# A Mamba-2 and attention block: segment sums taken as differences of running sums in one fp32r pass, and one convolution input projected later

## The chip, the cores and the metric

The kernel runs on one NeuronCore of a Trainium2 chip. The metric is the device time of one execution in microseconds (us), the median of several runs; lower is better. Five engines work side by side, each with its own instruction queue, and meet only through semaphores: TensorE (PE, with its weight loads as PEld), VectorE (DVE), ScalarE (ACT), GpSimd (POOL) and SyncE (SP, which here only issues DMAs).

## The reference

For each of 8 sequences of 512 tokens with 128 channels, after one layer norm, two branches are computed and joined as `x + s * silu(f)`:

```
s branch: h = layernorm(x); z, xBC, dt = h @ in_proj          (256 | 384 | 4 columns)
          xBC = silu(conv4(xBC)); xs, B, C = xBC;  dt = softplus(dt + bias)
          per head:  H_t = exp(dt_t * A) H_(t-1) + dt_t x_t B_t;   y_t = H_t C_t + D x_t
          y = rmsnorm(y * silu(z)) @ out_proj; + residual; then layernorm and a GELU MLP
f branch: rmsnorm, causal attention with 16 heads of 8 channels, then 4 experts, the top 2 weighted
```

The recurrence over t is done in 4 chunks of 128 tokens. Inside a chunk, with the running sum `S_t = sum of dt_k * A for k up to t` of one head, the weight of source token s for target token t is `exp(S_t - S_s)` for s up to t, times `C_t . B_s`. The exponent `S_t - S_s` is what the code calls the segment sum. There are 4 heads, so one chunk has a 128 x 512 tile of segment sums (source token on the partitions, head and target token on the free axis).

## The kernel before, in words

One sequence is one round. `stage_b(r, tail, head)` ends round r (its "tail": output projections, MLP, experts) and begins round r+1 (its "head": qkv, convolution and gate projections, maxima of the attention scores), interleaved by hand. `stage_a` then does the attention and the scan of the new round. The program is `stage_b(-1)` with head only, `stage_a`, seven loop rounds of `stage_b` and `stage_a`, and a last `stage_b` with tail only. The order of work on every engine is the order written in the code.

`stage_a` walks 24 units `e`, six (`u` = 0 to 5) for each of 4 quarters `g`. A unit is a slice of the attention scores: PE computes it (`exp_scores`, or two at once in `exp_scores_of_four`), ACT exponentiates it (`exponentiate`, L1097) into `pr`, POOL masks it (L1715), PE multiplies it with the values three units later (`weigh_values`). In quarter 0 the last maxima of the scores are still found: PE writes `max_scores`, DVE reduces them (`maxima`, L1194). The scan of chunk g is woven between: `segments` and `scan_inputs` at u = 1 (at e = 2 for chunk 0), then ACT's exponential of the segment sums into `es` (L1132), DVE's `scan_weights` (`wm`, L1474), PE's `scan_outputs` at u = 4.

Segment sums before: POOL's `decays(c)` (L1699) builds `rs`, 128 x 512, with row k, head h, column t holding `dta[k, h]` if k is at most t and else 0; `decays(0)` stands ahead of unit 0, the others at u = 3 of quarters 0 to 2. PE then multiplies with the constant `after` (1 where k > s), in fp32:

```
mm(R[1][:, :], after, rs[:, c % 2].rearrange("p h t -> p (h t)")).then_inc(seg_ps, 1)
```

In this trace every fp32 product of TensorE stands as two matmul instructions, and an fp32r or bf16 product as one. The running sums for the other uses come from `cumulate`, three small products into `S[0]` near the end of `stage_b`; ACT's exponential of them is `dec` (L1120). After `cumulate` PE does `experts_down(0)`, then `exp_scores(0)`, `max_scores` and so on; `experts_down(t)` uses the PSUM bank `R[(22 + t) % 4]`, so t = 3 uses `R[1]`, the bank of the segment sums. `rs` shares its memory with `h2a`, an expert's hidden activations.

At the start of `stage_b` PE's order is: qkv products, turning of `ao`, `project_x(0)`, the `wo` product, `project_x(1)`, `project_x(2)`, `project_z(0)`, `project_z(1)`, turning of `x1n`, `project_z(2)`, turning of `xf`, `project_z(3)`, gate logits, and 32 transposes of `tokqk` (L449). `project_x(n)` makes convolution input n, which ACT's `evac_xc(n)` copies out; ACT does `evac_xc(2)` after the squares and the root for `xf`.

Of the kernel before, what the change touches and what calls it, by code (L numbers as in the profile page):

```python
# [93 lines left out]
def build(nc, x, weights, vectors, rows, consts, out):  # L94
    with ExitStack() as ctx:
# [83 lines left out]
        rs = sb("rs", [P, 2, NH, P])  # L179
        es = sb("es", [P, 2, NH, P])  # L180
        gm = sb("gm", [P, 2, P])
# [30 lines left out]
        h2a = rs[:].rearrange("p k h t -> p k (h t)")  # L212
        h2b = es[:].rearrange("p k h t -> p k (h t)")
        h1a = wm[:].rearrange("p k h t -> p k (h t)")
        h1 = sb("h1", [P, 2, L])
        h3a = sb("h3a", [P, L])
# [55 lines left out]
        cum_ps = signal("cum_ps", 1)  # L272
        seg_ps = signal("seg_ps", T)
# [31 lines left out]
        dec_sb = signal("dec_sb", 1)  # L305
        seg_sb = signal("seg_sb", T)
# [29 lines left out]
        sv_sb = signal("sv_sb", 1)  # L336
        moe_sb = signal("moe_sb", T * E)
# [19 lines left out]
        rs_sb = signal("rs_sb", T)  # L357
# [84 lines left out]
        def _(pe):  # L442
# [128 lines left out]

            def segments(r, c):

                pe.wait_ge(rs_sb, at(rs_sb, r, c + 1))
                if c == 0:
                    pe.wait_ge(moe_sb, at(moe_sb, r, 4 * E))
                elif c == 1:
                    pe.wait_ge(h_sb, at(h_sb, r, 1))
                else:
                    pe.wait_ge(h_sb, at(h_sb, r, 2 * c - 1))  # L580
                mm(R[1][:, :], after, rs[:, c % 2].rearrange("p h t -> p (h t)")).then_inc(seg_ps, 1)
# [114 lines left out]
            def stage_b(r, tail, head):  # L696
# [36 lines left out]
                if head:  # L733
                    project_x(r, 1)
                    project_x(r, 2)
# [8 lines left out]
                if head:  # L744
                    project_z(r, 2)
# [95 lines left out]
                if head:  # L841
                    exp_scores(r, 0)
# [54 lines left out]
            pe.wait_ge(pool_set, 10)  # L897
            pe.wait_ge(dve_set, 7)
# [13 lines left out]
        def _(act):  # L912
# [201 lines left out]
            def stage_a(r, tail):  # L1114
# [37 lines left out]
            act.wait_ge(pool_set, 3)  # L1152
            act.preload_act_table_set(EXP_LN)
# [17 lines left out]
        def _(dve):  # L1171
# [145 lines left out]
            def stage_b(r, tail, head):  # L1317
# [91 lines left out]
                if tail:  # L1409
                    for n in range(2):  # L1410
# [7 lines left out]
                       ALU.add).then_inc(sv_sb, 1)  # L1418
                for t in range(T):
# [11 lines left out]
                    if head and t < 2:  # L1431
                        maxima(r, MAX_AT[t])

# [117 lines left out]
            dve.wait_ge(dve_set, 3)  # L1551
# [7 lines left out]
            dve.wait_ge(dve_set, 7)  # L1559
# [17 lines left out]
        def _(pool):  # L1577
# [80 lines left out]
            def time_steps(r):  # L1658
# [29 lines left out]
                pool.sem_inc(pool_passed, 1)  # L1688
                pool.wait_ge(rs_sb, at(rs_sb, r, 0))
# [3 lines left out]
            def decays(r, c, tail):  # L1693

                pool.wait_ge(dt_sb, at(dt_sb, r, DT_STEPS))
                if c == 0 and tail:
                    pool.wait_ge(up_ps, at(up_ps, r, 9))
                pool.wait_ge(seg_ps, at(seg_ps, r, c - 1))
                tt(rs[:, c % 2], upto.unsqueeze(1).broadcast_to([P, NH, P]),  # L1699
                   dta[:, c, :].unsqueeze(2).broadcast_to([P, NH, P]), ALU.mult).then_inc(rs_sb, 1)  # L1700

            def stage_a(r, tail):
                decays(r, 0, tail)
                for e in range(G * UNITS):
# [21 lines left out]
                    if u == 3 and g < T - 1:  # L1726
                        decays(r, g + 1, tail)
# [12 lines left out]
            pool.memset(xc[:, :, 0:3], 0.0).then_inc(pool_set, 1)  # L1740
            pool.memset(cT[:], 0.0).then_inc(pool_set, 1)
# [8 lines left out]
            pool.wait_ge(dve_set, 7)  # L1750
# [71 lines left out]
```

## Time and profile before

| | us |
|---|---|
| median of 3 runs | 872.43 |
| lowest, highest | 872.13, 874.5 |
| the profiled execution, its own time | 876.48 |
| its span (first to last instruction) | 874.8 |
| PE busy | 796.5 |
| DVE busy | 605.7 |
| ACT busy | 496.4 |
| POOL busy | 365.4 |

The profiled execution took 4 us more than the median; 1.7 us of it lie around the span. Busy times of PE are modelled, and a matmul's duration holds its way through the array, so the durations of two neighbours overlap. Start times are counted from the start of the span. The mean granted clock of TensorE over the span is 0.981 of 2.4 GHz.

### The profile page before, as it was taken

The page shows a single profiled execution, that of the slowest core. Times are in us where ns is not written, and L with a number is a line of the kernel's source. Part 1 is how long each engine was busy: PE and PEld are TensorE (multiplying, and loading weights), DVE is VectorE, ACT ScalarE, POOL GpSimd, SP SyncE. Part 2 cuts the span into 40 slices and gives each one's busy share as a digit, 9 for nine tenths or more (in the row PEclk, how much of TensorE's full clock was granted, in tenths as well). Part 3 has the DMA queues.
Part 4 walks back from the last instruction along what each step waited for, and adds up shares of the span by engine and source line. Part 5 has one row for each costly group of instructions (what it writes and reads, how often), then busy time and mean ns, then how long its engine had stood idle before and what let it go on. Part 6 is the DMA issues. An engine that isn't in the chain of part 4 may idle for free. (4 is left out here: it accounts for less than half of the span.)

```text
span 874.8 us, 18230 instructions
## 1 busy us (share of the span) xinstructions
PE 796.5 (91%) x5472; PEld 492.2 (56%) x5472; DVE 605.7 (69%) x1443; ACT 496.4 (57%) x952; POOL 365.4 (42%) x656
## 2 busy tenths in 40 slices
PE   2789999999999999999899999999999998999897
PEld 1554564755647556565647555475555656475555
DVE  2576469784787757786687847877587866878534
ACT  2325774467743675547744678436854577446652
POOL 5633627054541627227280454516272272804500
PEclk9897999999999998999999999999999999999999
DMA  4000000000000100000000000000000000000000
GB/s 163 1 3 18 14 1 1 9 16 25 0 1 6 33 5 0 7 12 25 0 0 7 13 24 0 1 7 26 11 0 7 12 26 0 0 7 13 24 1 13
DMA packets 15145, 11.73 MB, mean 13 GB/s; under 512 B 1040, under 2 KB 13968, under 8 KB 14992
## 3 DMA queue, kind: packets, MB, share of 16 engines
q1 hardware_dynamic: 15120, 11.43, 4.3%
q8 instruction: 12, 0.20, 0.1%
q14 instruction: 13, 0.11, 0.0%
HBM read 7.76 MB, written 2.10 MB: 11 GB/s over the span
## 5 line engine op out<-in xcount | busy, mean ns | idle before, releaser
L1097 ACT ACTIVATE sb_pr<-S 128x768 f32<-128x768 f32 (+1 forms) x192 | 165.8, 890 | 130.8 <-PE S L444 130.8
L1194 DVE TENSOR_REDUCE sb_mx<-S 128x2 f32<-128x256 f32 (+3 forms) x256 | 197.7, 816 | 41.7 <-PE S L444 41.1
L1715 POOL TENSOR_SCALAR_AFFINE_SELECT sb_pr<-sb_pr 128x256 f32<-128x256 f32 (+1 forms) x192 | 98.9, 517 | 292.7 <-ACT sb_pr L1097 289.4
L444 PE MATMUL R<-sb_pr,sb_va 128*32 128x512 f32 (+3 forms) x1024 | 89.7, 445 | 0.0
L444 PE MATMUL S<-sb_kT,sb_qT 32*128 32x256 f32 (+3 forms) x512 | 56.8, 386 | 19.7 <-DVE sb_mx L1194 15.8
L444 PE MATMUL R<-sb_W,sb_pr 128*128 128x96 f32 (+1 forms) x512 | 69.5, 276 | 0.0
L444 PE MATMUL R<-sb_xfT,sb_W 128*128 128x512 f32 x144 | 69.2, 602 | 0.0
L444 PEld LDWEIGHTS S<-sb_kT,sb_qT 32*128 32x128 f32 x512 | 27.8, 184 | 73.0 <-DVE sb_mx L1194 65.2
L444 PEld LDWEIGHTS R<-sb_W,sb_pr 128*128 128x128 f32 x512 | 63.5, 192 | 3.8 <-issue 3.5
L1655 POOL TENSOR_TENSOR sb_cv<-sb_cv,sb_cm 128x512 f32<-128x512 f32 x48 | 62.5, 1302 | 4.0
L444 PE MATMUL S<-sb_qT,sb_kT 32*128 32x256 f32 (+3 forms) x512 | 56.8, 387 | 5.6 <-ACT sb_pr L1097 4.8
L1428 DVE SCALAR_TENSOR_TENSOR sb_x<-R,sb_wts,sb_x 128x96 f32<-128x96 f32 x128 | 40.6, 317 | 22.9 <-PE R L444 19.5
L444 PEld LDWEIGHTS S<-sb_qT,sb_kT 32*128 32x128 f32 x512 | 27.6, 184 | 46.1 <-ACT sb_pr L1097 22.1
L444 PE MATMUL S<-sb_maskb,sb_identb 128*128 128x128 bf16 (+1 forms) x384 | 49.6, 242 | 0.0
L962 ACT ACTIVATE sb_pr<-R 128x512 f32<-128x512 f32 x32 | 19.1, 598 | 39.8 <-PE R L444 39.7
L1617 POOL TENSOR_TENSOR sb_qk<-sb_qk,sb_wqk 128x512 f32<-128x512 f32 x8 | 10.2, 1270 | 72.5 <-ACT sb_sq L997 72.5
L449 PE MATMUL S<-sb_cst,sb_tokqk 128*128 128x128 f32 x256 | 38.2, 321 | 2.4 <-DVE sb_tokqk L1380 2.2
L444 PE MATMUL R<-sb_rs,sb_cst 128*128 128x512 f32 x64 | 36.7, 656 | 2.9 <-DVE sb_x L1428 2.9
L1652 POOL TENSOR_SCALAR sb_cm<-sb_xc,sb_vec 128x512 f32<-128x512 f32 x48 | 36.3, 757 | 6.6 <-POOL sb_cv L1655 6.6
L444 PEld LDWEIGHTS R<-sb_pr,sb_va 128*32 128x32 f32 x1024 | 23.6, 108 | 27.2 <-issue 11.1
L449 PEld LDWEIGHTS S<-sb_cst,sb_tokqk 128*128 128x128 f32 x256 | 36.6, 171 | 3.3 <-DVE sb_tokqk L1380 2.6
L1182 DVE RECIPROCAL sb_rden<-R 128x16 f32<-128x16 f32 x32 | 8.2, 257 | 40.0 <-PE R L712 30.6
(216 smaller groups left out, 1711.2 us busy)
## 6 DMA issues: line engine op xcount, KB each, us to landing
sb_xin<-x SPq DMA_DIRECT2D x9, 256.0 KB, 2.7
sb_W<-weights SPq DMA_DIRECT2D x1, 2290.0 KB, 9.9
sb_qT<-sb_mT SPq DMA_DIRECT2D x128, 4.0 KB
sb_xres<-x SPq DMA_DIRECT2D x8, 256.0 KB, 2.8
out<-sb_xres SPq DMA_DIRECT2D x7, 256.0 KB, 2.3
sb_cT<-sb_xact SPq DMA_DIRECT2D x8, 128.0 KB, 2.3
sb_W<-weights SPq DMA_DIRECT2D x1, 514.0 KB, 4.6
sb_cst<-consts SPq DMA_DIRECT2D x1, 328.0 KB, 3.0
```

Source lines behind the costliest of these rows:

```text
L444: return pe.matmul(o, lhsT, rhs, start=start, stop=stop, skip_group_check=True)
L449: i = pe.transpose(o[:, t * P:(t + 1) * P], src(t), ident)
L962: act.activation(dst, R[k % 4][:, :], func, bias=bias).then_inc(act_up, 1)
L1097: act.activation(pr[:, e % 4, :, 0:n], S[pair_of_exp(e)][:, :, 0:n], ACT.Exp).then_inc(p_sb, 1)
L1182: dve.reciprocal(rden[:], view[:, :, :, HD]).then_inc(done, 1)
L1194: o = dve.tensor_reduce(mx[:, n // P - 1, g, heads[0]:heads[1] + 1], found[:, :, at_col:at_col + n], AX.X, ALU.max, negate=True)
L1428: stt(out=x2[:, t, MASKED:D], in0=R[(22 + t) % 4][:, e * OC:(e + 1) * OC], scalar=wts[:, t, e:e + 1], in1=x2[:, t, MASKED:D], op0=ALU.mult ...
L1617: tt(qk[:, :, 0].rearrange("p t h d -> p t (h d)"), qk[:, :, 0].rearrange("p t h d -> p t (h d)"), wqk[:].rearrange("p h d -> p (h d)").un ...
L1652: ts(cm[:], xc[:, n, k:k + L], vec[:, tap:tap + 1], 0.0, ALU.mult, ALU.add).then_inc(conv_pool, 1)
L1655: tt(cv[:, n], cv[:, n], cm[:], ALU.add).then_inc(conv_pool, 1)
L1715: pool.affine_select(out=keep, in_=keep, compare_op=ALU.is_ge, fill=0.0, base=0, pattern=pattern, channel_multiplier=-1)\
```

## The change

The segment sum is now formed as a difference. DVE's `sums_in_parts` takes the running sums that `cumulate` left in PSUM (16 columns: chunk and head), and stores each twice over as a part rounded to fp32r and a rest, into `cs` (128 tokens x 128, 32 columns for a chunk). PE turns `cs` with one transpose (`turn_sums`), so that parts lie on partitions: of each chunk's 32 partitions the first 8 and the next 8 hold the parts. By a scale and a bias per partition ACT makes from it `seg_v` (the parts on the first 8 of each chunk's partitions, ones on the next 8) and four `seg_l[c]` (ones on chunk c's first 8 partitions, the negated parts on its next 8, zero elsewhere); POOL spreads `seg_v` over the heads once, into `seg_r`. A chunk's segment sums are then one fp32r product of `seg_l[c]` and `seg_r`, and a bf16 product that adds the mask (-1e30 where s > t). So PE's `segments` has no operand that is made anew for each chunk, and POOL's four `decays` in a round become one product. `h2a` has memory of its own, `experts_down(3)` waits until ACT has read the turned sums out of `R[1]`, and `project_x(2)` stands after the turning of `x1n`. Six small reductions on DVE and a memset on POOL are added to the setup.

```diff
--- before.py
+++ after.py
-        rs = sb("rs", [P, 2, NH, P])
         es = sb("es", [P, 2, NH, P])
+        cs = sb("cs", [P, T, 32])
+        seg_v = sb("seg_v", [P, P])
+        seg_l = sb("seg_l", [P, T, P], F32R)
+        seg_r = sb("seg_r", [P, NH, P], F32R)
+        seg_low = sb("seg_low", [P, T])
+        seg_high = sb("seg_high", [P, T])
+        seg_sums = sb("seg_sums", [P, 2])
+        seg_head = sb("seg_head", [P, NH])
...
-        h2a = rs[:].rearrange("p k h t -> p k (h t)")
         h2b = es[:].rearrange("p k h t -> p k (h t)")
         h1a = wm[:].rearrange("p k h t -> p k (h t)")
         h1 = sb("h1", [P, 2, L])
+        h2a = sb("h2a", [P, 2, L])
...
+            def turn_sums(r):
+                pe.wait_ge(cs_sb, at(cs_sb, r, 2))
+                pe.wait_ge(act_up, at(act_up, r, 17))
+                pe.transpose(R[1][:, 0:P], cs[:].rearrange("p c k -> p (c k)"), ident).then_inc(csT_ps, 1)
+
             def segments(r, c):
 
-                pe.wait_ge(rs_sb, at(rs_sb, r, c + 1))
+                pe.wait_ge(segl_sb, at(segl_sb, r, 1 + T))
+                pe.wait_ge(segr_sb, at(segr_sb, r, 1))
                 if c == 0:
                     pe.wait_ge(moe_sb, at(moe_sb, r, 4 * E))
                 elif c == 1:
                     pe.wait_ge(h_sb, at(h_sb, r, 1))
                 else:
                     pe.wait_ge(h_sb, at(h_sb, r, 2 * c - 1))
-                mm(R[1][:, :], after, rs[:, c % 2].rearrange("p h t -> p (h t)")).then_inc(seg_ps, 1)
+                mm(R[1][:, :], seg_l[:, c, :], seg_r[:].rearrange("p h t -> p (h t)"), True, False)
+                mm(R[1][:, :].rearrange("p (h t) -> p h t", h=NH), maskb[:],
+                   identb[:].unsqueeze(1).broadcast_to([P, NH, P]), False, True).then_inc(seg_ps, 1)
...
+                if t == 3 and head:
+                    pe.wait_ge(segl_sb, at(segl_sb, r, 1 + T))
...
                 if head:
                     project_x(r, 1)
-                    project_x(r, 2)
                     project_z(r, 0)
                     project_z(r, 1)
                 if tail:
...
                         dense(bank(0)[:, 0:256], 2)
                 if head:
+                    project_x(r, 2)
                     project_z(r, 2)
...
+                    turn_sums(r)
                     exp_scores(r, 0)
                     max_scores(r, MAX_AT[0])
                     mask_scores(r, MAX_AT[0])
...
+                    if e == 0:
+                        act.wait_ge(csT_ps, at(csT_ps, r, 1))
+                        act.wait_ge(segr_sb, at(segr_sb, r, 0))
+                        act.activation(seg_v[:], R[1][:, 0:P], ACT.Identity, bias=seg_sums[:, 1:2],
+                                       scale=seg_sums[:, 0:1]).then_inc(segl_sb, 1)
+                        act.wait_ge(seg_ps, at(seg_ps, r, 0))
+                        for c in range(T):
+                            act.activation(seg_l[:, c, :], R[1][:, 0:P], ACT.Identity, bias=seg_low[:, c:c + 1],
+                                           scale=seg_high[:, c:c + 1]).then_inc(segl_sb, 1)
...
+                if head:
+                    sums_in_parts(r)
...
+            def sums_in_parts(r):
+
+                total = S[0][:, 0, 0:T * NH].rearrange("p (c h) -> p c h", h=NH).unsqueeze(2)\
+                    .broadcast_to([P, T, 2, NH])
+                parts = cs[:, :, 0:16].rearrange("p c (x y h) -> p c x y h", x=2, y=2)
+                dve.wait_ge(dec_sb, at(dec_sb, r, 1))
+                dve.wait_ge(csT_ps, at(csT_ps, r, 0))
+                dve.tensor_copy(parts[:, :, :, 0].bitcast(F32R), total).then_inc(cs_sb, 1)
+                dve.wait_ge(cs_sb, at(cs_sb, r, 1))
+                tt(parts[:, :, :, 1], total, parts[:, :, :, 0], ALU.subtract).then_inc(cs_sb, 1)
...
+            by_part = ident.rearrange("p (c k) -> p c k", c=T)
+            dve.tensor_reduce(seg_low[:], by_part[:, :, 0:8], AX.X, ALU.add).then_inc(dve_set, 1)
+            dve.tensor_reduce(seg_high[:], by_part[:, :, 8:16], AX.X, ALU.add, negate=True).then_inc(dve_set, 1)
+            dve.wait_ge(dve_set, 4)
+            dve.tensor_reduce(seg_sums[:, 0:1], seg_low[:], AX.X, ALU.add).then_inc(dve_set, 1)
+            dve.tensor_reduce(seg_sums[:, 1:2], seg_high[:], AX.X, ALU.add, negate=True).then_inc(dve_set, 1)
+            dve.tensor_reduce(sp[:, 0], by_part[:, :, 0:16].rearrange("p c (m h) -> p c h m", h=NH),
+                              AX.X, ALU.add).then_inc(dve_set, 1)
+            dve.wait_ge(dve_set, 7)
+            dve.tensor_reduce(seg_head[:], sp[:, 0].rearrange("p c h -> p h c"), AX.X,
+                              ALU.add).then_inc(dve_set, 1)
...
-            def decays(r, c, tail):
-
-                pool.wait_ge(dt_sb, at(dt_sb, r, DT_STEPS))
-                if c == 0 and tail:
-                    pool.wait_ge(up_ps, at(up_ps, r, 9))
-                pool.wait_ge(seg_ps, at(seg_ps, r, c - 1))
-                tt(rs[:, c % 2], upto.unsqueeze(1).broadcast_to([P, NH, P]),
-                   dta[:, c, :].unsqueeze(2).broadcast_to([P, NH, P]), ALU.mult).then_inc(rs_sb, 1)
-
             def stage_a(r, tail):
-                decays(r, 0, tail)
+                pool.wait_ge(segl_sb, at(segl_sb, r, 1))
+                pool.sem_inc(pool_passed, 1)
+                pool.wait_ge(seg_ps, at(seg_ps, r, 0))
+                tt(seg_r[:], seg_v[:].unsqueeze(1).broadcast_to([P, NH, P]),
+                   seg_head[:].unsqueeze(2).broadcast_to([P, NH, P]), ALU.mult).then_inc(segr_sb, 1)
...
-                    if u == 3 and g < T - 1:
-                        decays(r, g + 1, tail)
...
+            pool.memset(cs[:], 0.0).then_inc(pool_set, 1)
```

## Rows read from the trace of the kernel before

**Rows 1.** The page: busy time and share, and TensorE's granted clock in 40 slices.
```profile
PE 796.5 (91%) x5472; PEld 492.2 (56%) x5472; DVE 605.7 (69%) x1443; ACT 496.4 (57%) x952; POOL 365.4 (42%) x656
...
PEclk9897999999999998999999999999999999999999
```
**Rows 2.** Groups by line and form, whole span: names, shapes, count, busy us, mean ns.
```profile
L1699 POOL TENSOR_TENSOR sb_rs<-sb_cst,sb_dta 128x512 f32<-128x512 f32 x32 | 33.3, 1039 | 1.2 <-POOL sb_dta L1690 1.1
...
L444 PE MATMUL S<-sb_maskb,sb_identb 128*128 128x128 bf16 x256 | 28.5, 224 | 0.0
...
L444 PE MATMUL S<-sb_maskb,sb_identb 128*128 128x256 bf16 x128 | 21.1, 278 | 0.0
...
L444 PE MATMUL S<-sb_kT,sb_qT 32*128 32x512 f32 x128 | 20.4, 497 | 2.5 <-DVE sb_mx L1194 1.5 <-DVE sb_kT L1388 0.9
...
L444 PE MATMUL S<-sb_kT,sb_qT 32*128 32x384 f32 x128 | 18.3, 445 | 10.9 <-DVE sb_mx L1194 10.0
```
**Rows 3.** Timeline of the middle of a stage_b: start us, us, engine, line, operation.
```profile
547.34 1.88 PE L444 MATMUL R<-sb_rs,sb_W 128*128 128x512 f32 x4
...
549.06 1.02 PE L444 MATMUL R<-sb_x1T,sb_W 128*128 128x512 f32 x2
```
**Rows 4.** Timeline of ACT in quarter 2 of a stage_a; brackets are idle time.
```profile
501.08 1.02 ACT L1097 ACTIVATE sb_pr<-S 128x1024 f32<-128x1024 f32 x1 [2.56 <-PE S L444]
...
503.40 0.62 ACT L937 ACTIVATE sb_oT<-R 128x512 f32<-128x512 f32 x1
503.88 0.63 ACT L1132 ACTIVATE sb_es<-R 128x512 f32<-128x512 f32 x1
...
504.75 1.55 ACT L1097 ACTIVATE sb_pr<-S 128x768 f32<-128x768 f32 x2
506.86 1.51 ACT L1097 ACTIVATE sb_pr<-S 128x768 f32<-128x768 f32 x2 [0.56 <-PE S L444]
```
**Rows 5.** Timeline of PE in the same quarter: the segment sums.
```profile
502.11 1.13 PE L444 MATMUL R<-sb_rs,sb_cst 128*128 128x512 f32 x2
```
**Rows 6.** Timeline from the end of a stage_b through quarter 0, three engines.
```profile
472.53 0.21 ACT L1120 ACTIVATE sb_dec<-S 128x48 f32<-128x48 f32 x1 [3.27 <-PE S L444]
474.74 1.02 ACT L1097 ACTIVATE sb_pr<-S 128x1024 f32<-128x1024 f32 x1 [2.00 <-PE S L444]
...
475.62 1.21 DVE L1194 TENSOR_REDUCE sb_mx<-S 128x2 f32<-128x1024 f32 x1
...
484.60 0.69 DVE L1474 TENSOR_TENSOR sb_wm<-sb_es,sb_gm 128x512 f32<-128x512 f32 x1 [0.30 <-ACT sb_es L1132]
...
486.08 1.12 DVE L1527 TENSOR_SCALAR sb_xn<-sb_xin,sb_mv,sb_lnv 128x128 f32<-128x128 f32 x2
...
482.76 1.10 PE L444 MATMUL R<-sb_rs,sb_cst 128*128 128x512 f32 x2 [0.42 <-DVE sb_x L1428]
```
**Rows 7.** Timeline of PE in the first third of a stage_b.
```profile
533.30 0.66 PE L449 MATMUL R<-sb_cst,sb_xf 128*128 128x128 f32 x4 [1.18 <-DVE sb_xf L1364]
```
**Rows 8.** Timeline of the 32 transposes in two rounds, and ACT's dec in three.
```profile
330.61 6.44 PE L449 MATMUL S<-sb_cst,sb_tokqk 128*128 128x128 f32 x32
...
535.83 3.71 PE L449 MATMUL S<-sb_cst,sb_tokqk 128*128 128x128 f32 x32
...
163.94 0.21 ACT L1120 ACTIVATE sb_dec<-S 128x48 f32<-128x48 f32 x1 [3.27 <-PE S L444]
...
371.20 0.21 ACT L1120 ACTIVATE sb_dec<-S 128x48 f32<-128x48 f32 x1 [3.21 <-PE S L444]
...
778.16 0.21 ACT L1120 ACTIVATE sb_dec<-S 128x48 f32<-128x48 f32 x1 [3.26 <-PE S L444]
```
**Rows 9.** Windows, first round: PE, PEld, DVE, ACT, POOL busy, then granted clock.
```profile
66.00:68.00 2.00, 1.48 (x8) 0.64 (x6) 1.23 (x1) 1.11 (x2) 0.42 (x1) 0.65 0.09 19
...
70.00:72.00 2.00, 2.00 (x8) 1.08 (x8) 1.56 (x5) 0.81 (x1) 0.42 (x2) 0.50 0.00 0
```
**Rows 10.** Timeline of the setup: POOL's last memset.
```profile
7.52 0.39 POOL L1742 MEMSET sb_hst<- 128x256 f32 x1
```

More of the change, by code:

```diff
@@ L272, in build @@
         cum_ps = signal("cum_ps", 1)
+        csT_ps = signal("csT_ps", 1)
         seg_ps = signal("seg_ps", T)
@@ L305, in build @@
         dec_sb = signal("dec_sb", 1)
+        segl_sb = signal("segl_sb", 1 + T)
         seg_sb = signal("seg_sb", T)
@@ L336, in build @@
         sv_sb = signal("sv_sb", 1)
+        cs_sb = signal("cs_sb", 2)
         moe_sb = signal("moe_sb", T * E)
@@ L356, in build @@
         spa_sb = signal("spa_sb", 3)
-        rs_sb = signal("rs_sb", T)
+        segr_sb = signal("segr_sb", 1)
         pm_sb = signal("pm_sb", G * UNITS)
@@ L896, in _ @@
             pe.wait_ge(c_loaded, 48)
-            pe.wait_ge(pool_set, 10)
-            pe.wait_ge(dve_set, 7)
+            pe.wait_ge(pool_set, 11)
+            pe.wait_ge(dve_set, 13)
             pe.wait_ge(xab_sb, at(xab_sb, -2, 1))
@@ L1152, in _ @@
             act.wait_ge(pool_set, 3)
+            act.wait_ge(dve_set, 6)
             act.preload_act_table_set(EXP_LN)
@@ L1548, in _ @@
             dve.tensor_copy(maskb[:], future).then_inc(dve_set, 1)
+            by_part = ident.rearrange("p (c k) -> p c k", c=T)
[9 more added lines that the diff above has]
+                              ALU.add).then_inc(dve_set, 1)
             ts(wqk[:], row[:, R_QN:R_QN + HD].unsqueeze(1).broadcast_to([P, AH, HD]), HD ** -0.5, None,
                ALU.mult).then_inc(dve_set, 1)
-            dve.wait_ge(dve_set, 3)
+            dve.wait_ge(dve_set, 9)
             tt(wqk[:], wqk[:], row[:, R_KN:R_KN + HD].unsqueeze(1).broadcast_to([P, AH, HD]),
@@ L1558, in _ @@
             norms(-2)
-            dve.wait_ge(dve_set, 7)
+            dve.wait_ge(dve_set, 13)
             stage_b(-1, False, True)
@@ L1687, in time_steps @@
                 pool.wait_ge(cum_ps, at(cum_ps, r, 0))
-                pool.sem_inc(pool_passed, 1)
-                pool.wait_ge(rs_sb, at(rs_sb, r, 0))
                 tt(dta[:], dt[:], neg_a[:].unsqueeze(1).broadcast_to([P, T, NH]),
                    ALU.mult).then_inc(dt_sb, 1)
-            def decays(r, c, tail):
-                pool.wait_ge(dt_sb, at(dt_sb, r, DT_STEPS))
-                if c == 0 and tail:
-                    pool.wait_ge(up_ps, at(up_ps, r, 9))
-                pool.wait_ge(seg_ps, at(seg_ps, r, c - 1))
-                tt(rs[:, c % 2], upto.unsqueeze(1).broadcast_to([P, NH, P]),
-                   dta[:, c, :].unsqueeze(2).broadcast_to([P, NH, P]), ALU.mult).then_inc(rs_sb, 1)
-            def stage_a(r, tail):
-                decays(r, 0, tail)
+            def stage_a(r, tail):
+                pool.wait_ge(segl_sb, at(segl_sb, r, 1))
[3 more added lines that the diff above has]
+                   seg_head[:].unsqueeze(2).broadcast_to([P, NH, P]), ALU.mult).then_inc(segr_sb, 1)
                 for e in range(G * UNITS):
@@ L1749, in _ @@
             pool.sem_inc(pool_passed, 1)
-            pool.wait_ge(dve_set, 7)
+            pool.wait_ge(dve_set, 13)
             pool.sem_inc(pool_passed, 1)
```

## The prediction

> **What bounds the kernel.** The page says that PE is busy 91% of the span, far ahead of DVE at 69% and ACT at 57% [rows 1]. Read as a share of the whole, every PE cycle saved would be time saved. So I went to the groups by form, for the cost of the segment product, and then to the timelines of single quarters, to see what is waiting when that product ends.
>
> A round is some 101.3 us: `dec` starts at 371.20 and again at 472.53 [rows 6, 8]. In quarter 2 of a stage_a ACT works from 501.08 to 506.30 (504.75 + 1.55) with no idle bracket: two exponentials, between and behind them the turned y, `oT`, `es` and the squares, then two more exponentials in 1.55 us. The only waits for PE are before the first (2.56 us) and before the next pair at 506.86 (0.56) [rows 4]. The segment product of this quarter runs from 502.11 to 503.24 [rows 5], and its reader `es` starts at 503.88 because `oT` is before it on ACT [rows 4]. It has 0.6 us to spare. So in quarters 1 to 3 this stretch is set by ACT, and PE is busy without being the bound. In quarter 0 the segment product at 482.76 had waited 0.42 us for the last expert sum of DVE, and DVE's `wm` at 484.60 waits 0.30 us for `es` [rows 6]: here the product is nearly on the path. The early part of stage_b is a chain over DVE and ACT, in which PE idles; before the transposes of `xf` it has been idle 1.18 us [rows 7].
>
> **The clock.** The slices show the granted clock below full speed early on and once in the middle [rows 1]. The 32 transposes behind that idle stretch take 3.71 us in the round of 535.83 but 6.44 us in the round of 330.61 [rows 8]: the second ran at 1.2 GHz. Seven `dec`s, the first at 163.94 and the last at 778.16, are 614.2 us apart [rows 8]; six rounds of 101.33 would be 608.0. The other 6.2 us are what the falls of the clock at this place cost in this execution (the transposes above alone account for 2.7 of them). In the first round too the clock falls, in the window from 66 to 68 us, after the stall around the start of stage_a, and is at half from 70 to 72 [rows 9].
>
> **The change part by part.**
>
> *Segment product.* Before: two instructions of 512 columns in fp32. Four such in a row take 1.88 us and two 1.02 [rows 3], so two more cost 0.86 us, which is one product. After: an fp32r instruction of 512 columns grows by 497 - 445 = 52 ns for 128 columns, and a bf16 one by 278 - 224 = 54 ns [rows 2], so 0.21 us each and 0.43 together. The fp32r rows have 32 partitions and not 128; I take the same rate. Bounds for the pair: 0.43, and 0.86 if the full array takes fp32r at half that rate and the two don't overlap well. So 0.43 us of PE time is saved in each of 32 products, 13.7 us in all, and nothing at the far bound. How much is on the path:
> - Quarters 1 to 3 (24 products): 0. ACT's unbroken run hides it; if that cover were gone it would be 24 x 0.43 = 10.3 us.
> - Quarter 0 of the seven loop rounds: `es` comes 0.4 us earlier, `wm` takes up its 0.30 wait, and the maxima behind `wm` on DVE start earlier, until they meet scores that PE has not finished. I read the slack as about 0.13 of 0.30: 7 x 0.13 = 0.9 us. Bounds 0 and 7 x 0.30 = 2.1.
> - Quarter 0 of the first round: at half clock [rows 9] the saving doubles to 0.85 us, and PE goes straight on to the next scores: -0.85.
>
> *`turn_sums`.* One transpose, 3.71 / 32 = 0.12 us [rows 8], ahead of `exp_scores(0)`. It needs the two small DVE operations behind `dec`, which ends at 472.74; taking 0.21 us for each, as `dec` itself has, and a little for two hops, they end at about 473.3. PE is then still in `experts_down(0)`: the scores behind it let ACT start only at 474.74, after 2.00 us idle [rows 6]. The 0.12 us of PE is hidden as well: the second block of maxima waits for DVE's maximum of the first, 475.62 + 1.21 = 476.83 [rows 6], and that does not move. DVE's copies fall into idle time before its first expert sum. So 0 in loop rounds; 7 x 0.12 = 0.8 if the cover fails. In the first round there is no `experts_down(0)` to cover it: `exp_scores(0)`, which ran before `dec`, now waits for `dec`, two DVE operations and a transpose. I put it at +1.0 once (bounds 0.5 and 2, from one small operation's delay to the whole chain at half clock).
>
> *Five small ACT operations* of 128 columns after the first exponential. The nearest rows are `dec` with 48 columns, 0.21 us [rows 6], and `oT` with 512, 0.62 [rows 4]. I take 0.35 each with their two pointers, 1.75 in all (bounds 1.05 and 3.1). The first exponential ends at 475.76 [rows 6], so the second, which now comes behind them, starts at 477.5 (at the far bound 478.9). PE needs it just before the segment product of 482.76 [rows 6]: cost 0. `experts_down(3)`, which now waits for the same copies, ends with the expert sum that DVE adds just before 482.76, and so starts some 3 us earlier, 2 us after the copies.
>
> *POOL.* Four products of 1.04 us [rows 2] become one, behind `seg_v` at about 476.2. POOL's first mask is late by under 2 us; the first product with the values, which needs it, comes after the segment product of 482.76. Less work on POOL could also help DVE: its two `xn` ran beside `rs(1)` and took 1.12 us [rows 6]. No row shows them without a neighbour, so I take 0.06 us a round, 0.4 in all (0 to 1).
>
> *`project_x(2)`*, two instructions, 0.86 us on PE. It leaves a place where PE is early anyway, since next it has to wait for `x1n`, and goes into the 1.18 us before the transposes of `xf` [rows 7]. `evac_xc(2)` on ACT then starts some 0.3 us later; behind it ACT waits for the same transposes of `xf`. By its own time: 0. If ACT had no slack there: 7 x 0.3 = +2.1. But it divides the idle stretch. The falls of the clock come after that stretch, and PE has 0.86 us more work in it now. I take it that about half of the falls go: of the 6.2 us in the profiled execution some 3 to 4, and in the median one, which is 4 us faster than the profiled and so had fewer falls, 2.5. Bounds: 0 and 6.2. No row gives this; it is the weakest term.
>
> The Trainium skill, "TensorE: Matmul & The Clock Gate", Part 1: The HAM clock gate, says that the throttled state is the default and that activity releases it. By that rule the moved product helps here; the trace agrees that the clock falls behind idle PE and nowhere in the dense parts. The same rule speaks against the other half of the change, which takes work away from PE in stage_a (rival C).
>
> *Setup.* A memset of 128 columns on POOL, which is on the chain to the first `xa`: the one of 256 columns takes 0.39 [rows 10], so +0.2 once. The six DVE reductions lie in idle time of DVE.
>
> **The sum.** -0.9 - 0.85 + 1.0 + 0.2 - 0.4 = about -1.0 us without the clock, and -2.5 with it: -3.5. Made on the profiled execution it is 876.5 - 1.0 - 3.5 = 872; on the median 872.4 - 3.5 = 869.
>
> **The rivals.**
> - A: PE is the bound, as 91% says. Then 32 x 0.43 less 8 x 0.12 is 12.8 us: 859.5. Against it: ACT's unbroken run [rows 4]. The Trainium skill, "Perfetto Trace Analysis", Identifying the Most-Contended Engine, would have one optimize the engine of the highest occupancy first, while it warns of PE's busy time; by the rule alone 859.5 would be the time.
> - B: the clock's falls are only shifted, not fewer, and the quarter 0 gain is lost to the next wait. What is left is -1 to +1: 871.4 to 873.4.
> - C, the slower one: PE's emptier stage_a lets the clock fall there in loop rounds, as it did in the first round [rows 9]. One fall costs about half its length. At 1.6 us a fall (a quarter of the 6.2 us) the time is 871.4 + 1.6 n with stage_b's falls left as they are: 882.6 for one in each of seven rounds, slower than before from the first on and by over 0.3% from the third. Against it: quarters 1 to 3 already hold idle PE before the change and never show it.
>
> **Numbers.** Forecast 0.50, B 0.32, A 0.06, C 0.12. A run of this kernel tells no change from about 0.3%, 2.6 us, so faster is below 869.8 and slower above 875.0. The forecast lies at 864.5 to 869.8 for the most part, B within 0.3%; of C some 0.09 is slower. Faster 0.56, same 0.35, slower 0.09. The range of 8 in 10 is 864.5 (872.4 - 2.1 for quarter 0 at its bound, and 5.8 of the 6.2 us of falls) to 873.5 (B's end).
>
> **What would show it.** Right: the segment product at about 0.45 us of PE; the stretch from first to fourth exponential of quarters 1 to 3 still 5.2 us, with PE's wait longer; `es` of quarter 0 0.4 us earlier and `wm` without wait; transposes of `tokqk` at 3.7 us in more rounds, with rounds of 101.2. Wrong: a quarter of under 9.4 us would mean that PE was the bound; a second exponential after 478 or a PE wait at `turn_sums` in loop rounds a new cost; a granted clock of 0.5 in a loop round's stage_a rival C.

## The result, and the profile after

The changed kernel takes 872.86 us in the median of 20 runs, the kernel before 874.77 in 20 runs beside them; the ratio is 0.9967 [0.9953, 0.9981]. One run of the changed kernel (1449.54 us, although its record shows a granted clock of 1.0) and one of e2 (1080.14 us) stand far outside all others: the ratios leave them out, the medians given do not (without them 872.84 and 878.49). The medians lie 1.9 us apart, and the ratio is worth 2.9. On the 872.43 of the first three runs the ratio gives 869.6 us, for 869.0 predicted; those three lay 2.3 us below the later median of their own kernel, and 872.86 as it stands is 3.9 above the forecast. The profiled execution took 874.18 us with a span of 872.5. Two things happened: an undisturbed round is 0.21 us shorter, and the falls of TensorE's clock (stretches at its lower level, 1.2 GHz) left stage_b, but others came in quarter 0 of stage_a.

The page and the groups by form, against [rows 1, 2]:

```profile
PE 785.0 (90%) x5480; PEld 483.2 (55%) x5480; DVE 601.9 (69%) x1465; ACT 510.2 (58%) x992; POOL 338.5 (39%) x633
...
PEclk9997999999999999999999999999999999999999
```
```profile
L454 PE MATMUL R<-sb_seg_r,sb_seg_l 128*128 128x512 f32 x32 | 16.1, 502 | 2.9 <-DVE sb_x L1461 2.9
...
L1153 ACT ACTIVATE sb_seg_l<-R,sb_seg_low,sb_seg_high 128x128 fp32r<-128x128 f32 x32 | 12.0, 469 | 0.0
```

PE lost 11.5 us of busy time and POOL 26.9, and the kernel gained 2 to 3. The slices hide the clock here: no digit in the middle is below 9, and yet four loop rounds hold a fall.

Quarter 2 of a round without a fall, ACT, against [rows 4]:

```profile
703.27 1.02 ACT L1118 ACTIVATE sb_pr<-S 128x1024 f32<-128x1024 f32 x1 [2.56 <-PE S L454]
...
705.59 0.62 ACT L958 ACTIVATE sb_oT<-R 128x512 f32<-128x512 f32 x1
706.07 0.63 ACT L1162 ACTIVATE sb_es<-R 128x512 f32<-128x512 f32 x1
...
709.04 1.51 ACT L1118 ACTIVATE sb_pr<-S 128x768 f32<-128x768 f32 x2 [0.55 <-PE S L454]
```

The quarter did not move at all: from the first exponential to `es` 2.80 us (2.80 before), to the last pair 5.77 (5.78 before), and the waits are the same.

From `dec` through quarter 0 of the same kind of round, three engines, against [rows 6]:

```profile
674.86 0.21 ACT L1141 ACTIVATE sb_dec<-S 128x48 f32<-128x48 f32 x1 [3.21 <-PE S L454]
677.24 1.02 ACT L1118 ACTIVATE sb_pr<-S 128x1024 f32<-128x1024 f32 x1 [2.17 <-PE S L454]
678.16 0.45 ACT L1149 ACTIVATE sb_seg_v<-R,sb_seg_sums 128x128 f32<-128x128 f32 x1
678.50 1.50 ACT L1153 ACTIVATE sb_seg_l<-R,sb_seg_low,sb_seg_high 128x128 fp32r<-128x128 f32 x4
679.87 1.05 ACT L1118 ACTIVATE sb_pr<-S 128x1024 f32<-128x1024 f32 x1
...
685.91 0.60 ACT L1162 ACTIVATE sb_es<-R 128x512 f32<-128x512 f32 x1 [0.52 <-PE R L454]
...
686.55 0.68 DVE L1518 TENSOR_TENSOR sb_wm<-sb_es,sb_gm 128x512 f32<-128x512 f32 x1
687.39 0.96 DVE L1225 TENSOR_REDUCE sb_mx<-S 128x2 f32<-128x768 f32 x1 [0.15 <-PE S L454]
688.26 0.59 DVE L1571 TENSOR_SCALAR sb_xn<-sb_xin,sb_mv,sb_lnv 128x128 f32<-128x128 f32 x2
...
685.09 0.47 PE L454 MATMUL R<-sb_seg_r,sb_seg_l 128*128 128x512 f32 x1 [0.42 <-DVE sb_x L1461]
685.40 0.39 PE L454 MATMUL R<-sb_identb,sb_maskb 128*128 128x512 bf16 x1
685.72 0.44 PE L454 MATMUL S<-sb_qT,sb_kT 32*128 32x384 f32 x2
```

The pair of products holds PE for 0.63 us (685.09 to 685.72). ACT's five small operations take 1.71 us from the first to the next exponential. `wm` has no wait any more, and the maximum behind it now waits 0.15 us for PE's scores: this is the next wait, and it ends the gain.

Stage_b of one round, against [rows 7, 8], and three starts of `dec`:

```profile
634.37 0.66 PE L459 MATMUL R<-sb_cst,sb_xf 128*128 128x128 f32 x4 [0.32 <-DVE sb_xf L1395]
...
636.91 3.71 PE L459 MATMUL S<-sb_cst,sb_tokqk 128*128 128x128 f32 x32
```
```profile
163.76 0.21 ACT L1141 ACTIVATE sb_dec<-S 128x48 f32<-128x48 f32 x1 [3.21 <-PE S L454]
266.33 0.21 ACT L1141 ACTIVATE sb_dec<-S 128x48 f32<-128x48 f32 x1 [3.21 <-PE S L454]
...
775.98 0.21 ACT L1141 ACTIVATE sb_dec<-S 128x48 f32<-128x48 f32 x1 [3.21 <-PE S L454]
```

The idle time before the transposes of `xf` is 0.32 us for 1.18, and the 32 transposes take 3.71 us in every loop round. But the round from 163.76 to 266.33 takes 102.57 us, and the three after it 102.46 to 102.49; the last two take 101.11 and 101.12. The place is quarter 0. PE in the round of 163.76, and windows of 2 us there (columns as in [rows 9]):

```profile
174.00 0.47 PE L454 MATMUL R<-sb_seg_r,sb_seg_l 128*128 128x512 f32 x1 [0.41 <-DVE sb_x L1461]
...
174.63 0.44 PE L454 MATMUL S<-sb_qT,sb_kT 32*128 32x384 f32 x2
175.59 0.44 PE L454 MATMUL S<-sb_kT,sb_qT 32*128 32x384 f32 x2 [0.52 <-DVE sb_mx L1225]
...
176.18 1.94 PE L454 MATMUL R<-sb_pr,sb_va 128*32 128x512 f32 x8
```
```profile
174.00:176.00 2.00, 1.48 (x7) 0.66 (x8) 2.00 (x5) 1.47 (x4) 0.99 (x2) 1.00 0.00 0
176.00:178.00 2.00, 2.00 (x12) 0.28 (x10) 1.61 (x4) 0.63 (x2) 0.41 (x1) 0.54 0.00 0
```

The same place before the change (its round of 163.94):

```profile
174.18 1.10 PE L444 MATMUL R<-sb_rs,sb_cst 128*128 128x512 f32 x2 [0.41 <-DVE sb_x L1428]
175.21 0.44 PE L444 MATMUL S<-sb_qT,sb_kT 32*128 32x384 f32 x2
175.78 0.44 PE L444 MATMUL S<-sb_kT,sb_qT 32*128 32x384 f32 x2
...
176.37 1.07 PE L444 MATMUL R<-sb_pr,sb_va 128*32 128x512 f32 x8
```
```profile
174.20:176.20 2.00, 1.87 (x7) 0.67 (x8) 1.70 (x5) 1.08 (x3) 0.99 (x2) 1.00 0.02 4
176.20:178.20 2.00, 2.00 (x22) 0.97 (x21) 2.00 (x3) 1.35 (x3) 1.34 (x2) 1.00 0.00 0
```

The scores at 175.59 wait for DVE's maximum, which does not come earlier (they start 11.83 us after `dec`, and 11.84 before the change), so the 0.40 us that the shorter product saves turn into idle PE: 1.48 us busy of 2 for 1.87. Right behind it the granted clock falls to 0.54 of full speed, near the 1.2 GHz level, and the same eight products of the values take 1.94 us and not 1.07. Rounds with such a fall are 1.34 to 1.45 us longer than those without.

### The profile page after: what moved, and what is told of

Its sections match the earlier page's. It is cut to its first block and busy times, and to the rows that moved or that the text cites. A ratio compares the mean times of both kernels' runs of the same rounds, so it can differ in the third digit from the quotient of the medians.

```text
span 872.5 us, 18294 instructions
## 1 busy us (share of the span) xinstructions
PE 785.0 (90%) x5480; PEld 483.2 (55%) x5480; DVE 601.9 (69%) x1465; ACT 510.2 (58%) x992; POOL 338.5 (39%) x633
## 5 line engine op out<-in xcount | busy, mean ns | idle before, releaser
L454 PE MATMUL R<-sb_pr,sb_va 128*32 128x512 f32 (+3 forms) x1024 | 93.2, 459 | 2.8 <-POOL sb_pr L1763 1.6
L1750 POOL TENSOR_TENSOR sb_seg_r<-sb_seg_v,sb_seg_head 128x512 fp32r<-128x512 f32 x8 | 8.3, 1039 | 135.9 <-ACT sb_seg_v L1149 135.9
L454 PEld LDWEIGHTS S<-sb_maskb,sb_identb 128*128 128x128 bf16 x384 | 23.9, 98 | 21.6 <-issue 17.8
L1530 DVE TENSOR_TENSOR sb_yc<-R,sb_dec 128x256 f32<-128x256 f32 x24 | 10.2, 425 | 35.8 <-PE R L454 35.8
```

What stands on the lines that cost most here:

```text
L454: return pe.matmul(o, lhsT, rhs, start=start, stop=stop, skip_group_check=True)
L1530: tt(yc[:, 0, :].rearrange("p (h d) -> p h d", h=NH), R[3][:, DI:2 * DI].rearrange("p (h d) -> p h d", h=NH), dec[:, 0, c, :].unsqueeze(2) ...
L1750: tt(seg_r[:], seg_v[:].unsqueeze(1).broadcast_to([P, NH, P]), seg_head[:].unsqueeze(2).broadcast_to([P, NH, P]), ALU.mult).then_inc(segr_ ...
```

## The experiments

All in one table. "e1" to "e12" are further kernels, made from the kernel before (e1, e11, e12) or from the changed one (the others). "Round" is the length of a loop round without a fall, from `dec` to `dec`; "falls" are those of the loop rounds in the one profiled execution, in quarter 0 of stage_a and in stage_b.

| kernel | us, median (runs) | ratio to before | round | falls a, b |
|---|---|---|---|---|
| before | 874.77 (20) | | 101.33 | 0, 3 |
| changed | 872.86 (20) | 0.9967 [0.9953, 0.9981] | 101.12 | 4, 0 |
| e1 move only | 869.3 (6) | 0.9933 [0.9906, 0.9959] | 101.34 | 0, 0 |
| e11 the same again | 872.13 (9) | 0.9965 [0.9951, 0.9980] | 101.42 | 0, 1 |
| e2 sums only | 879.21 (12) | 1.0039 [1.0012, 1.0066] | 101.16 | 3, 2 |
| e3 one filler | 870.8 (7) | 0.9945 [0.9924, 0.9966] | 101.14 | 0, 2 |
| e4 two fillers in quarter 0 | 876.66 (12) | 1.0012 [0.9996, 1.0028] | 101.93 | 0, 1 |
| e5 POOL's products back | 872.33 (1) | | 101.13 | 5, 0 |
| e6 product twice, quarters 1 to 3 | 874.49 (1) | | 101.18 | 4, 0 |
| e7 turning later | 875.13 (12) | 0.9999 [0.9979, 1.0019] | 101.52 | 4, 0 |
| e8 e3, and a filler in stage_b | 869.15 (6) | 0.9939 [0.9915, 0.9963] | 101.15 | 0, 1 |
| e9 product twice, quarter 0 | 869.51 (6) | 0.9921 [0.9905, 0.9938] | 101.11 | 2, 1 |
| e10 e8 with one filler more | 867.99 (6) | 0.9923 [0.9900, 0.9945] | 101.14 | 0, 0 |
| e12 move and fillers, old sums | 868.77 (6) | 0.9920 [0.9899, 0.9941] | 101.63 | 0, 0 |

The first interval, named below, is that from the first `dec` to the second. How many falls an execution has varies from run to run, so one profile is a sample; the ratios are over all runs of a line, but for the two named above. The intervals of all kernels with a ratio under 0.995 overlap, so these ratios do not rank them.

**e1: the moved input alone**, on the kernel before.

```diff
                     project_x(r, 1)
-                    project_x(r, 2)
...
                 if head:
+                    project_x(r, 2)
                     project_z(r, 2)
```

> The kernel before with only the third convolution input moved. Theory: the move keeps the clock up in the early stage_b, where it fell in three loop rounds of the kernel before, and changes nothing else. So no loop round has the 32 transposes above 4 us, the undisturbed round stays at 101.33 us, and the time falls to 7 x 0.21 = 1.5 us above the best runs of the changed kernel (869.2): about 871, ratio 0.995 to 0.997. Rival (the falls of the clock depend only on when they happen to come, and the move does nothing): ratio 1.000, and falls in some stage_b as before.

Rounds of 101.34 and not one fall in a loop round. First and last `dec` of the loop:

```profile
163.88 0.21 ACT L1120 ACTIVATE sb_dec<-S 128x48 f32<-128x48 f32 x1 [3.26 <-PE S L444]
...
771.94 0.21 ACT L1120 ACTIVATE sb_dec<-S 128x48 f32<-128x48 f32 x1 [3.27 <-PE S L444]
```

These 608.06 us were 614.22 before [rows 8]. The moved product costs nothing by itself in this execution, which has no fall. The ratio, 0.9933, is below the expected 0.995 to 0.997, and no worse than that of the whole change.

**e2: the sums alone**, the changed kernel with `project_x(2)` at its old place.

> The changed kernel with the third convolution input at its old place. Theory: the segment sums alone give 0.21 us in each loop round (undisturbed rounds of 101.1 us) but open a place in quarter 0 of stage_a where the clock can fall, and the falls in the early stage_b come back. So 1.5 us gained and falls at both places: ratio 0.998 to 1.003, slower than the changed kernel by 2 to 4 us. Rival: the move is without effect, so this is as fast as the changed kernel, ratio 0.997.

Slower than before, by 0.39% [0.12, 0.66], a little more than the expected range allows, although its undisturbed round (101.16) is shorter than 101.33. It has both kinds of falls. So the new sums by themselves cost more clock than they save work, and the move pays for them.

**e3: a filler in quarter 0**, on the changed kernel: two products of constants, 256 columns each, into a free bank, ahead of the wait for the last expert sum. `dense` is the kernel's own filler, which it uses in the first and last stage_b.

```diff
                 if c == 0:
+                    pe.wait_ge(moe_sb, at(moe_sb, r, 2 * E))
+                    dense(R[3][:, 0:256], 2)
                     pe.wait_ge(moe_sb, at(moe_sb, r, 4 * E))
```

> The changed kernel with two more products of 256 columns (fp32, 0.43 us of PE, result unused) just before PE waits for the last expert sum ahead of the first segment product, where it has 0.41 us idle. Theory: the clock fell in quarter 0 because PE had too little to do between 172.9 and 176; the filler puts back the 0.4 us that the cheaper product took out, costs nothing in time, and the falls there go. Ratio to the kernel before 0.993 to 0.995 (869 us). Rival (the falls in quarter 0 have to do with the phase only): ratio stays 0.997; and if the filler is not hidden, rounds are 0.4 us longer, ratio 1.000.

No fall in stage_a any more; two in stage_b. PE in a loop round:

```profile
476.55 1.08 PE L454 MATMUL R<-sb_cst 128*128 128x256 f32 x4
477.29 0.58 PE L454 MATMUL R<-sb_seg_r,sb_seg_l 128*128 128x512 f32 x1
...
478.73 0.44 PE L454 MATMUL S<-sb_kT,sb_qT 32*128 32x384 f32 x2 [0.26 <-DVE sb_mx L1227]
```

The filler holds PE for 0.74 us (476.55 to 477.29), more than the wait of 0.41 and than the 0.43 expected for it: the product behind it starts 0.15 us later after `dec` (10.39 for 10.24). The round grows by 0.02 us only, since the next scores wait for DVE anyway. In the first round, at half clock, the filler is not hidden: the first interval is 99.09 us in e8, which has it there, and 97.78 in e10, which has not.

**e4: a second filler** in the other idle stretch of quarter 0, between the scores and the maxima of unit 3.

```diff
                             exp_scores(r, e)
+                            if e == 3:
+                                dense(R[3][:, 0:256], 2)
                             max_scores(r, MAX_AT[e])
```

> As the run with the filler, and two more such products in PE's 0.5 us wait for a maximum in the same quarter (between the fourth unit's scores and its maxima). Theory: if one filler isn't enough, this is; no falls in quarter 0, 869 us, ratio 0.993 to 0.995, undisturbed rounds of 101.1 us. Rival: the second filler is not hidden fully and costs 0.1 to 0.2 us in each of eight rounds, ratio 0.995 to 0.996.

A miss. The filler holds PE for 1.06 us where 0.26 were idle:

```profile
174.10 1.13 PE L454 MATMUL R<-sb_cst 128*128 128x256 f32 x4
175.16 0.44 PE L454 MATMUL S<-sb_kT,sb_qT 32*128 32x384 f32 x2
```

The maxima behind it come that much later, and each round pays 0.8 us. A filler that does not fit costs more than half a fall, and in every round.

**e5 and e6: where the 0.21 us a round come from, and whether the 24 products are free.** e5 is the changed kernel with one product of 128 x 512 back on POOL at u = 3 of quarters 0 to 2; e6 issues the fp32r product of quarters 1 to 3 twice.

```diff
+                    if u == 3 and g < T - 1:
+                        tt(seg_x[:], seg_v[:].unsqueeze(1).broadcast_to([P, NH, P]),
+                           seg_head[:].unsqueeze(2).broadcast_to([P, NH, P]), ALU.mult)
```
```diff
-                mm(R[1][:, :], seg_l[:, c, :], seg_r[:].rearrange("p h t -> p (h t)"), True, False)
+                for _ in range(2 if c else 1):
+                    mm(R[1][:, :], seg_l[:, c, :], seg_r[:].rearrange("p h t -> p (h t)"), True, False)
```

> The changed kernel with one more product of 128 x 512 on POOL at u = 3 of quarters 0 to 2, into memory that nothing reads; the rest is as changed. It splits the 0.21 us by which an undisturbed round of the changed kernel is shorter (101.12 for 101.33). My account by the rows after the change: most of it is the two `xn` of DVE in quarter 0, 0.59 us where they were 1.12, because POOL's product no longer lies beside them. Then this kernel has `xn` near 1.1 again and undisturbed rounds of 101.25 to 101.33. Rival: `es` 0.4 us earlier is the source and DVE's `xn` is hidden; then `xn` is near 1.1 and the rounds stay at 101.12.

> The changed kernel with the fp32r product of the segment sums issued twice in quarters 1 to 3, the second writing over the first, so that each of the 24 products is some 0.3 us longer on PE, about as long as the fp32 product was. The prediction gave these 24 products 0: then undisturbed rounds stay at 101.12. If PE is the bound there (rival A in small), each round is 0.9 us longer, 102.0. A half-way result would say that one or two of the three quarters have PE on the path. `es` of quarter 1 should come 0.3 later in either case.

Both are single executions. e5: DVE's two `xn` took 0.88 us beside POOL's product in the one round without a fall (0.66 to 0.88 over the rounds; 0.59 without it, 1.12 before), and the round stayed at 101.13: so far as the load on DVE came back, its relief is hidden. My account fell and its rival stood. e6: 101.17 to 101.19 for 101.12, that is 0.06 us for three products of 0.3: the prediction's zero was right to 0.02 us a product.

**e7: `turn_sums` behind `exp_scores(0)`.**

```diff
-                    turn_sums(r)
                     exp_scores(r, 0)
+                    turn_sums(r)
                     max_scores(r, MAX_AT[0])
```

> The changed kernel with `turn_sums` behind `exp_scores(0)` in PE's order; nothing else differs. In the first round `exp_scores(0)` then no longer waits for `dec` and DVE's two operations: the first exponential should start 0.5 to 1.0 us earlier against `dec`, which the prediction priced at +1.0, and the first interval be shorter by 0.3 to 0.8. In loop rounds the first exponential comes 0 to 0.1 us earlier and the rounds stay at 101.1. If the prediction's +1.0 was wrong (the second exponential, behind ACT's five small operations, sets the pace of the first round), the first interval stays at 98.8. Ratio to before: 0.996, as the change itself, with the falls of the clock as they happen.

The first interval is 97.87; in e5, whose order there is that of the change and whose clock was low for as long, it is 97.81. So nothing is won. The loop rounds lose 0.40 us (101.52 for 101.12), which I had not expected. PE in e7, then in the changed kernel:

```profile
469.55 0.50 PE L454 MATMUL S<-sb_qT,sb_kT 32*128 32x512 f32 x2
469.98 0.33 PE L585 MATMUL R<-sb_cst,sb_cs 128*128 128x128 f32 x1
470.24 0.50 PE L454 MATMUL S<-sb_kT,sb_qT 32*128 32x512 f32 x2
```
```profile
575.25 0.27 PE L585 MATMUL R<-sb_cst,sb_cs 128*128 128x128 f32 x1
575.45 0.50 PE L454 MATMUL S<-sb_qT,sb_kT 32*128 32x512 f32 x2
575.46 0.50 PE L454 MATMUL S<-sb_kT,sb_qT 32*128 32x512 f32 x2
```

The two pairs of 32-row products start 0.01 us apart in the changed kernel: they run side by side. With the full-array transpose between them they start 0.69 apart, one after the other. The Trainium skill, "TensorEngine Tiling (Array Packing)", Key Properties of its tiling modes, says that different tiles can work in parallel and that a change of the mode drains the engine; these rows agree with both.

**e8 and e10: fillers in stage_b too.** e8 is e3 with two products ahead of the wait for `x1n` (0.93 us idle). e10 leaves the filler of quarter 0 out of the first round and puts one product ahead of the wait for `xf`.

```diff
                 if tail:
+                    if head:
+                        dense(R[0][:, 0:256], 2)
                     pe.wait_ge(x1n_sb, at(x1n_sb, r, 1))
```

> The changed kernel with e3's two filler products ahead of the wait of the segment sums in quarter 0, and two more of the same size in stage_b ahead of the wait for `x1n`, where PE idles 0.93 us. If idle PE is what lets the clock fall, in each place where it idles, the falls in stage_a stay away as in e3 and those left in stage_b (two of them in e3) go as well: loop rounds of 101.1 to 101.3 without exception, 868.0 to 869.5, ratio 0.991 to 0.994. Rival: the fillers delay the transposes of `x1n` and the chain behind them, 0.1 us or more a round, or a fall stays in some round in spite of them: ratio 0.994 or more, as e3 alone.

> The kernel of e8 with the filler of quarter 0 left out of the first round, where it cost some time at half clock, and one filler more in stage_b, ahead of the wait for `xf` (0.32 us idle). If idle PE alone is behind the falls, the last fall in stage_b (one in e8) goes too; the first interval is 0.3 to 0.8 shorter than the 99.09 of e8; 867.5 to 868.5, ratio 0.990 to 0.993. Rival: a filler of 0.43 us does not fit the 0.32 us of idle, delays the turning of `xf`, and ACT and the gate behind it: rounds of 101.25 to 101.4 and a ratio of 0.994 or more.

e8 kept one fall in stage_b, so its expectation of none fell. e10 had none, and rounds of 101.11 to 101.17: even the last filler did not delay anything that counts. Its first interval is 1.31 us shorter than that of e8, where 0.3 to 0.8 was expected. First and last `dec` of its loop:

```profile
160.41 0.21 ACT L1148 ACTIVATE sb_dec<-S 128x48 f32<-128x48 f32 x1 [3.21 <-PE S L454]
...
767.24 0.21 ACT L1148 ACTIVATE sb_dec<-S 128x48 f32<-128x48 f32 x1 [3.21 <-PE S L454]
```

606.83 us for 612.22 in the changed kernel. Its median of 867.99 is the lowest of all, and both kernels of the study are above it; its interval overlaps those of e1, e3, e8, e9 and e12.

**e9: the fp32r product twice, in quarter 0 alone.**

```diff
+                for _ in range(1 if c else 2):
+                    mm(R[1][:, :], seg_l[:, c, :], seg_r[:].rearrange("p h t -> p (h t)"), True, False)
```

> The changed kernel with the fp32r product of the segment sums issued twice in quarter 0 alone, the second writing over the first; quarters 1 to 3 as changed. PE then has in quarter 0 about the work that it had before the change (the pair of fp32r products and the mask product some 0.94 us, for 1.03 before). Theory: the falls of the clock at quarter 0 come from the 0.3 to 0.4 us of work that the product lost there. Then no loop round has a fall in stage_a, undisturbed rounds are 101.2 to 101.35 (`es` later again), 869 to 870, ratio 0.993 to 0.996. Rival: what opened the idle time is not the shorter product but something else in the new order of quarter 0 (where the turning, the two waits at 0.42 and 0.53 us and the next scores fall); then falls in stage_a stay in two or more of the seven rounds and the ratio is 0.996 or more.

Mixed: two falls in stage_a by the profile, as the rival had it, but the ratio of 0.9921 is the theory's. The product and the wait behind it:

```profile
680.83 0.70 PE L454 MATMUL R<-sb_seg_r,sb_seg_l 128*128 128x512 f32 x2 [0.41 <-DVE sb_x L1462]
...
682.42 0.45 PE L454 MATMUL S<-sb_kT,sb_qT 32*128 32x384 f32 x2 [0.29 <-DVE sb_mx L1226]
```

0.23 us more work on PE (0.54 to the mask product for 0.31) makes the wait 0.29 us and not 0.53. Ordered by idle PE around this place: before the change 0.41 and about 0.1 us, no fall; e3, e8 and e10, none and 0.26, no fall; e9, 0.41 and 0.29, two; changed, e2, e5, e6 and e7, 0.41 and 0.53, three to five. It also bears on the 0.21 us: here `es` is only 0.16 us earlier than before the change, and the round is as short as with 0.39, so what `es` gains beyond 0.16 is worth nothing.

**e11: e1 once more**, beside e9 and e10 on one chip.

> The kernel of e1 once more (the kernel before with only the moved convolution input), beside the others on the same chip. The first look had no fall in any loop round, 869.3 us and 0.9933 from six runs. If this is the kernel's nature, again rounds of 101.33 throughout and 0.991 to 0.996. If the first look was luck and the falls of stage_b are only rarer, one or two rounds of 103 to 104.7 and 0.996 or more.

One fall and 0.9965. The move makes the falls of stage_b rare and does not end them. The two sets of runs put it at 3 to 6 us. The rounds of 101.42 were 101.34 in e1; the same code, so 0.08 us a round is how far executions on two chips lie apart.

**e12: the old sums with the move and the fillers of e10.**

> The old segment sums (fp32 product, four products on POOL) with the moved convolution input and the three fillers of e10: quarter 0 ahead of the segment sums' wait in loop rounds, and ahead of the waits for `x1n` and `xf` in stage_b. It separates what the fp32r sums are worth once the clock is held in either kernel. By the milestones of the undisturbed rounds (`es` 0.39 earlier, yet only 0.14 us kept from the third maximum on, and some 0.07 at the end) the sums give 0.2 to 0.3 us a round: rounds of 101.33 to 101.42 here against 101.14 in e10, no fall or one, 868.5 to 870.5, ratio 0.992 to 0.995. Rival: with the fp32 product behind it the filler of quarter 0 no longer fits in front of the wait and delays the next scores, so that the old sums lose 0.5 us or more a round: rounds of 101.8 or more, 872 or more.

Rounds of 101.61 to 101.64, between my value and the rival's. The fp32 product starts 10.58 us after `dec`, and 10.23 before the change: the filler delays it by 0.35 us, for 0.15 in e10, and behind the longer product this is no longer hidden. (One fall stands in the last stage_b, outside the loop.) In this pair the new sums are 0.49 us a round ahead (101.63 for 101.14), but part of that is the filler's delay in front of the longer product: without a filler they are 0.21 ahead (101.33 for 101.12), or 0.31 by e11 and e9 on one chip (101.42 for 101.11). In the median it is 0.8 us, 868.77 for 867.99, less than six runs can tell.

## Why the prediction was right, and for reasons partly wrong

- **Segment product**: 0.43 us saved each was predicted; 0.40 in quarter 0 (1.03 before, 0.63 after). Both prices were too low, 0.86 for 1.03 and 0.43 for 0.63, and it is luck that the errors cancel in the difference. 24 of them at zero: right, by the unmoved quarter 2 and by e6. PE's busy share would have promised 859.5 (rival A); it lost 11.5 us of work for 2 to 3 us of time. The rule of the Trainium skill, "Perfetto Trace Analysis", Identifying the Most-Contended Engine, to optimize the engine of the highest occupancy first, would not have led to the time here; its warning of PE's busy time fits.
- **Quarter 0**: `es` 0.4 earlier (0.39), `wm`'s wait of 0.30 gone, slack of 0.13 a round. Measured 0.15 at the next maximum and 0.14 from there on at every exponential, `es`, `x1n` and `xf` up to the end of stage_b, with 0.07 more before the next `dec` whose source I did not find. POOL's 0.06 a round, the term beside it, did not show in e5. Together -0.21 a round for -0.19.
- **`turn_sums` and the five ACT operations**: hidden, as said. The second exponential starts 5.01 us after `dec`, for 4.97 predicted; 1.71 us for 1.75.
- **First round and setup**: product -0.79 for -0.85; the product starts 0.69 us later after `dec` (6.22 for 5.53), for +1.0 predicted. The interval grew by 0.36 for 0.15 predicted; between e11 and e5, where the clock is low for equally long, it grew by 0.18 (97.63 to 97.81). Moving the turn (e7) did not bring it back. The +0.2 of the memset does not show: the first `dec` starts at 62.73 us in e11 and at 62.72 in e5, both at full clock up to it.
- **The clock**: here the prediction was wrong in both halves, and they cancelled. "About half of the falls go" was too few: all of stage_b's went in this profile, and the move alone gives 3 to 6 us for the 2.5 of the sum. And the sums' own part was forecast at -1.0 us; alone (e2) it is about +3.4 us (0.39% of 875). The missed step is rival C, which I held as a separate case at 0.12, dismissed because "quarters 1 to 3 already hold idle PE". It is not a case of its own but runs beside the forecast, and in quarter 0, where two waits lie within 2 us. Its price was 1.6 us a fall, a quarter of the 6.2; but the 6.2 were three falls, of 1.66, 1.64 and 2.94 us, the last at the low level for twice as long. Measured elsewhere 1.3 to 1.45 in quarter 0 and 1.6 to 1.75 in stage_b. Rival B, falls shifted and not fewer, describes the profiled executions best: 6.2 us of falls before, 5.5 after (612.22 less 6 x 101.12). That the sum came out near the measured ratio is to that extent luck.

Shown: the falls follow the idle PE at the two places, since filling each removes them or makes them rare (e3, e1, e10) and e2 brings both back. The Trainium skill, "TensorE: Matmul & The Clock Gate", Part 1: The HAM clock gate, has activity as what releases the throttle; the runs agree in that less work on PE brought falls (e2) and more kept them away (e3, e10), so the rule cut both ways, as the prediction said.

The traces also show why some rounds with the same idle time fall and others do not: it is a matter of when the idle time comes. The low stretches of one execution start on one regular beat. In the changed kernel the four in quarter 0 start at 176.15, 278.55, 380.95 and 483.35 us, 102.40 apart, which is 12.39, 12.22, 12.12 and 12.06 us after `dec`; a round with such a fall lasts 102.5, so one fall tends to bring the next, and the falls of an execution are not independent of each other. In the changed kernel, e2, e5 and e6 (28 loop rounds in all) quarter 0 falls in each of the 16 rounds in which the beat comes 12.03 to 12.44 us after `dec`, and in none of the 12 others. The cures can be read at the same places. With the filler of quarter 0 the beat comes at 12.08 (e3), 12.32 (e8) and 12.37 us (e10), with the old sums at 12.07 (before), 12.27 and 12.38 (e11), and none of these rounds falls. In stage_b the falls before the change start 62.51, 62.78 and 63.09 us after `dec`; with the moved product the beat comes at 62.59 to 63.06 in four rounds of e1 and e11 without a fall, and the one fall of e11 starts later, at 63.58. So it is the idle time, and not the beat alone, that the cures change. Open: why the low stretches start on such a beat, and how much idle time there is too much.

## What to carry to other kernels

Ask of every saving on PE what PE does in the time that comes free. Where the next instruction waits for another engine, the saving is idle time, and idle time next to another short wait can cost more by the clock than the work did. Cheap cures are to move work that is due anyway into the gap, or a filler of about the gap's length; a filler that is much longer costs its excess in every round. Since one fall can bring the next, take several executions before judging a cure. Look for falls round by round, by the interval of one recurring instruction, since the slices of the page can hide them all.

## What the runs showed of the hardware

- Among the runs of the changed kernel from 869 to 878 us the time follows the mean granted clock: 869.1 to 869.5 us with 0.988, 877.7 with 0.976. It is not so in every run: one of the kernel before, beside e1, took 875.9 us with 0.943.
- An fp32r product of 512 columns over the full array holds PE 0.31 us to the bf16 product behind it, which holds it 0.32; the fp32 product held it 1.03.
- A 128-column transpose between two pairs of 32-row products makes the second pair 0.57 us later after `dec` (2.28 for 1.71) than the same transpose ahead of both, which takes 0.20, since the pairs stop running side by side.
- DVE's two `xn` of 128 x 128 take 0.59 us alone, 0.66 to 0.88 (e5) or 1.12 (before) beside a POOL product of 128 x 512.
- The low level of TensorE's clock came in a loop round right behind idle stretches of PE of 0.41 and 0.53 us with 1.07 us of work between them (changed kernel), and cost 1.34 to 1.45 us.
